# Batch 0's mixing beside the position tables, key terms on four column groups, first stacks and tables in turn

## The chip, the cores and the metric

The kernel runs on one core of a Trainium2 chip, as one launch. The metric is the device time of the launch in microseconds. Engines are named as the profile names them: PE is TensorE's matmuls, PEld its weight loads, DVE is VectorE, ACT is ScalarE, POOL is GpSimd, SP is SyncE, which only issues DMAs.

## What is computed

One block of a vision tower on x of shape (32, 512, 256, 4): a mixing over the last two axes, attention with relative position terms in two directions (32 batches, 512 positions, 16 heads of 16), and a layer of eight experts. What the change touches:

```python
h = einsum('bhid,oi,od->bho', x, weighted_sum, weight)
n = layernorm(h)
q, k, v = n @ Wq + bq, n @ Wk + bk, n @ Wv + bv      # 16 heads of 16
re = layernorm(rel_emb) * ln_g + ln_b                # 128 positions
pos_k, pos_q = re @ Wpk + bpk, re @ Wpq + bpq
scores = (q k^T + take(q pos_k^T, rel) + take(k pos_q^T, -rel)^T) / sqrt(48)
ctx = softmax(scores) @ v
h = h + ctx @ Wo + bo
```

## The kernel before

The program is a row of stages, each one or more blocks; a block ends when all its engines have ended and its last transfers have landed. B is 32 batches, P is 128, QT = 4 tiles of 128 positions make a batch's S = 512, HC = 2 chunks of 128 make the H = 256 channels, NH is 16 heads.

**Tables** (first block of `project`, L222 to L328). SP issues 19 loads (L226) and then the inputs of batches 0 and 1 (L229), 2 MB each. DVE waits for all 19 loads, takes the statistics of the embedding (L257), makes the mixing weights (eight products of 128x256, L262, into `mix`), normalizes, and goes on in turns with PE: transposes (L307), projections (L312), end and table matmuls (L319, L320), then DVE splits the tables into three bf16 parts (L276 to L292), PE makes the low rows (L324) and the bias of the key terms (L326), DVE splits the low rows, SP stores (L233, L235). PE has nothing else to do in this block.

**Projection loop** (second block of `project`, from L363). For each batch n PE does, in this order: `turn` (transposes of the normalized rows, L415), then for each of four tiles the mixing of batch n + 1 (L404: eight matmuls of 128x128 weights and 256 columns into `m_h[:, t]`) with a quarter of the q and k projections (L425) between the tiles, then `key_terms` (L433) and `project_v` (L442, two halves that share `m_v`). Ahead of the loop PE mixes batch 0, in four tiles on its own. A matmul in the program on fp32 data is two MATMULs in the profile. Key terms are 32 rows (two sides of 16 heads) by 512 positions: a projection of `full_k` with `kterm_w`, written to 32 partitions. ACT evicts them twice (L507, L508), POOL subtracts (L555), DVE splits (L610, L612). ACT also evicts h (L477) and q and k; DVE takes statistics and normalizes the next batch (L583), for which POOL takes a power (L537). SP's order within a batch is fixed: input of batch n + 2 (L371), h (L374), v (L376), then, when the last part is split, 12 DMAs of the parts (L383, L384) and 2 of the key terms (L386, L387).

**Attention** (`attend`, from L706). For each of 512 heads: `tables` (PE multiplies the head's rows in `stack` with `tabs`, L859), ACT evicts them to `skew_in` (L941, two buffers), SP writes them to a ring in HBM (L738) and reads them back skewed (L750) into `bias`, POOL (L809, L818, L827) and DVE (L995) fill and mask, PE adds up the scores (L871, L873, L878), DVE adds the rest of the bias and takes the maximum (L1010, L1017), PE turns them (L887), ACT takes the exponential (L947), PE multiplies with the values (L900, four heads into four groups of 32 output partitions). Tables are made LEAD = 5 heads ahead, read back NEXT = 3 heads ahead; `stack` has SR = 8 slots of SH = 2 heads. `load_stack` and the other issues of SP stand in one order written out by hand. Before the loop SP loads the constants (L709 to L717), waits until DVE has set the ones rows of all eight slots (L982, L983), loads seven slots and the values, and then writes tables 0 to 4, with reads 0 to 2 after writes 2 to 4. PE waits for all constants and all ones.

**Output and experts** follow; the change does not touch them.

Of the kernel before, what the change touches and what calls it, by code (L numbers as in the profile page):

```python
# [17 lines left out]
BF16 = mybir.dt.bfloat16  # L18
I32 = mybir.dt.int32
U32 = mybir.dt.uint32  # L20
ALU = mybir.AluOpType
# [3 lines left out]
P = 128  # L25
# [128 lines left out]
def project(nc, io, B, ctx, sem, passed, d_tab, d_plain, d_stack, d_kterm, d_v, d_h):  # L154
# [12 lines left out]
    kterm_bias = sb("kterm_bias", [2 * NH, 1])  # L167
# [3 lines left out]
    x_in = [sem(f"p_x_in{u}") for u in range(2)]  # L171


    with ExitStack() as tctx:
# [3 lines left out]
        def tps(name, shape):  # L178
# [22 lines left out]
        t_tab = tps("tab", [P, 2 * HC, S])  # L201
        t_end = tps("end", [P, 2, HC, 2])
        t_low = tps("low", [2 * NH, 2 * TW])
        t_in, t_const, t_dve, t_pe, t_pool, t_out = (
            sem("t_" + n) for n in ("in", "const", "dve", "pe", "pool", "out"))
        loads = [
            (ws, io["wsT"].rearrange("(c p) o -> p c o", p=P)),
            (wd, io["tok_weight"].partition_broadcast(P)),
# [13 lines left out]
        with nc.Block() as block:  # L222
            @block.sync
            def _(sp):
                for dst, src in loads:
                    sp.dma_start(dst[:], src).then_inc(t_in, 16)  # L226
                for u in range(2):

                    sp.dma_start(xt[:, u], xT[u].rearrange("d (c p) s -> p (d c) s", p=P)).then_inc(x_in[u], 16)  # L229
# [15 lines left out]

            @block.vector
            def _(dve):
# [7 lines left out]

                dve.wait_ge(t_in, 16 * len(loads))
# [3 lines left out]
                for d in range(ND):  # L260
                    for c in range(HC):
                        nc.vector.tensor_tensor(mix[:, d * HC + c], ws[:, c], wd[:, d], ALU.mult)  # L262
# [41 lines left out]
            def _(pe):  # L304
                pe.wait_ge(t_dve, 6)
                for c in range(HC):
                    mm = pe.transpose(t_turn[:, c * P:(c + 1) * P], rel[:, c * P:(c + 1) * P], ident[:])  # L307
                mm.then_inc(t_pe, 1)
                pe.wait_ge(t_dve, 7)
# [4 lines left out]
                mm.then_inc(t_pe, 1)  # L314
                pe.wait_ge(t_dve, 8)
# [5 lines left out]
                mm.then_inc(t_pe, 1)  # L321
                pe.wait_ge(t_dve, 19)
                for c in range(HC):
                    pe.matmul(t_low[0:NH, 0:TW], own_low[:, c], tab_q[:, c], start=(c == 0), stop=(c == HC - 1))  # L324
                for c in range(HC):
                    mm = pe.matmul(t_low[:, TW:TW + 1], kterm_w[:, c], consts[:, 0, c, 0:1], start=(c == 0),  # L326
                                   stop=(c == HC - 1))
# [14 lines left out]
    full_t = sb("full_t", [2 * NH, S])  # L342
    part_t = sb("part_t", [2 * NH, 3, S], BF16)
    v_sb = sb("v_sb", [P, QT, NH, VROW])
    m_h = ps("m_h", [P, QT, H])
# [3 lines left out]
    m_t = ps("m_t", [2 * NH, S])  # L349
# [13 lines left out]
    with nc.Block() as block:  # L363
# [33 lines left out]
        def _(pe):  # L397
            def mixing(n, i, u, t):
# [7 lines left out]
                if t % 2:  # L406
                    mm.then_inc(h_done, 1)
# [52 lines left out]
            for t in range(QT):  # L460
                mixing(0, 0, 0, t)
# [1255 lines left out]
```

## Time and profile before

| | us |
|---|---|
| median of 3 runs (lowest, highest) | 5222.62 (5219.48, 5224.54) |
| profiled execution, its own time | 5222.77 |
| its span, first to last instruction | 5220.9 |
| tables and stores, to the next block | 0 to 48.1 |
| projection block | 48.1 to 977.1 |
| one batch in it (transposes begin at 887.52 and 915.71) | 28.2 |
| attention block | 977.1 to about 4350 |
| output, choice of rows and experts | to 5220.9 |

The launch adds 1.9 us to the span. The granted clock of TensorE is 0.945 of full on the mean, 0.50 in the stretches in which it had been idle. In the views below, times are from the span's start; "idle before" is the time the engine stood still ahead of a group, and the name behind the arrow is what ended it.

### The profile page before, as it was taken

The numbers are of one execution on the slowest core, as the hardware profiler recorded it, in microseconds if no ns is written. First come the engines' busy times: TensorE is split into PE (matmuls) and PEld (weight loads), VectorE is DVE, ScalarE is ACT, GpSimd is POOL, SyncE is SP. The second block draws the span as 40 slices with busy tenths as digits, with TensorE's granted clock in tenths as the row PEclk, the third lists the DMA queues.
The fourth block names the chain that finished last, engine by engine and source line by source line (L and its number), as shares of the span: only waits on it lengthen the run. The fifth ranks groups of instructions, "written<-read, shape, count | busy, mean of one in ns | idle before, by whom it ended". The sixth has DMA issues, their size and how long they took to land. (4 is left out here: it accounts for less than half of the span.)

```text
span 5220.9 us, 110891 instructions
## 1 busy us (share of the span) xinstructions
PE 4618.7 (88%) x31272; PEld 3293.2 (63%) x31272; DVE 3524.1 (67%) x9058; ACT 2584.8 (50%) x4809; POOL 1925.2 (37%) x4461
## 2 busy tenths in 40 slices
PE   6999999499999999999999999999999996771698
PEld 4666666276666666666666666666666664661565
DVE  3333333388888878888878878888888885775511
ACT  1222222266666666666666666666666661110011
POOL 1222222144444444444444444444444443550022
PEclk9999999799999999999999999999999997885599
DMA  4766767699999999999999999999999995771033
GB/s 137 237 225 223 235 223 231 212 349 353 351 340 348 343 331 351 346 336 347 343 328 344 353 332 342 345 337 346 339 342 344 350 340 168 250 241 61 9 90 73
DMA packets 672172, 1461.31 MB, mean 280 GB/s; under 512 B 48195, under 2 KB 290291, under 8 KB 671603
## 3 DMA queue, kind: packets, MB, share of 16 engines
q1 hardware_dynamic: 665462, 1446.22, 81.7%
q0 software_dynamic: 6144, 8.52, 1.0%
q8 instruction: 236, 3.87, 0.3%
q14 instruction: 330, 2.70, 0.2%
HBM read 738.61 MB, written 715.94 MB: 279 GB/s over the span
## 5 line engine op out<-in xcount | busy, mean ns | idle before, releaser
L1010 DVE CUSTOM_DVE_ANT_1 a_scored<-a_ps_m_s,a_bias 128x512 f32<-128x512 f32 x2048 | 1397.5, 682 | 575.2 <-PE a_ps_m_s L878 543.5
L947 ACT ACTIVATE a_probsT<-a_ps_m_t 128x512 f32<-128x512 f32 x2048 | 1227.1, 605 | 938.3 <-PE a_ps_m_t L887 936.3
L887 PE MATMUL a_ps_m_t<-a_ident,a_scored 128*128 128x128 f32 x8192 | 1264.5, 277 | 0.5 <-ACT a_probsT L947 0.5
L941 ACT ACTIVATE a_skew_in<-a_ps_m_tab 128x512 f32<-128x512 f32 x2048 | 1125.7, 614 | 199.7 <-DMA d_skew<-a_skew_in 140.5
L887 PEld LDWEIGHTS a_ps_m_t<-a_ident,a_scored 128*128 128x128 f32 x8192 | 938.9, 141 | 437.3 <-DVE a_scored L1017 352.1
L1017 DVE TENSOR_SCALAR a_scored<-a_scored,a_top_of 128x512 f32<-128x512 f32 x2048 | 1045.2, 530 | 0.0
L827 POOL TENSOR_SCALAR_AFFINE_SELECT a_bias<-a_bias 128x128 f32<-128x128 f32 (+2 forms) x2560 | 980.5, 410 | 71.9 <-POOL a_bias L827 63.1
L818 POOL COPY a_bias<-a_high 128x128 f32<-128x128 f32 (+1 forms) x1024 | 355.9, 376 | 1764.9 <-DMA a_bias<-d_skew 1763.6
L878 PE MATMUL a_ps_m_s<-a_ident,a_bias 128*128 128x128 f32 x5120 | 902.6, 273 | 0.0
L859 PE MATMUL a_ps_m_tab<-a_tabs,a_stack 96*128 96x256 bf16 (+1 forms) x4096 | 714.2, 276 | 192.5 <-ACT a_skew_in L941 122.2
L878 PEld LDWEIGHTS a_ps_m_s<-a_ident,a_bias 128*128 128x128 f32 x5120 | 683.4, 142 | 109.0 <-issue 3.1
L873 PE MATMUL a_ps_m_s<-a_stack 99*128 99x512 bf16 (+2 forms) x2048 | 701.5, 343 | 45.5 <-issue 25.4
L859 PEld LDWEIGHTS a_ps_m_tab<-a_tabs,a_stack 96*128 96x128 bf16 (+1 forms) x4096 | 336.6, 98 | 411.0 <-ACT a_skew_in L941 344.7
L995 DVE COPY_PREDICATED a_bias<-a_ps_m_past,a_high 128x384 f32<-128x384 int32 x1024 | 544.1, 586 | 37.5 <-POOL a_high L809 34.0
L900 PE MATMUL a_ps_m_ctx<-a_probsT,a_values 128*17 128x512 f32 x4096 | 542.7, 602 | 1.2 <-ACT a_ctx_sb L953 1.2
L404 PE MATMUL p_ps_m_h<-p_mix,p_xt 128*128 128x256 f32 x2048 | 465.3, 381 | 7.3 <-PEq L222 7.3
L404 PEld LDWEIGHTS p_ps_m_h<-p_mix,p_xt 128*128 128x128 f32 x2048 | 388.7, 191 | 99.0 <-issue 51.9
L873 PEld LDWEIGHTS a_ps_m_s<-a_stack 99*128 99x128 bf16 x2048 | 200.6, 98 | 120.4 <-issue 64.5
L871 PE MATMUL a_ps_m_s<-a_stack 102*128 102x128 bf16 (+1 forms) x1024 | 254.7, 249 | 0.0
L1190 PE MATMUL o_ps_m_o<-o_wo,o_ctxn 128*128 128x256 f32 x512 | 166.8, 498 | 68.1 <-POOL o_ctxn L1156 68.0
L547 POOL TENSOR_TENSOR p_rest_q<-p_full_q,p_part_q 128x512 f32<-128x512 f32 x64 | 90.4, 1412 | 329.2 <-ACT p_part_q L496 329.2
L1190 PEld LDWEIGHTS o_ps_m_o<-o_wo,o_ctxn 128*128 128x128 f32 x512 | 128.6, 257 | 97.2 <-POOL o_ctxn L1156 40.4
(182 smaller groups left out, 3641.8 us busy)
## 6 DMA issues: line engine op xcount, KB each, us to landing
d_skew<-a_skew_in SPq DMA_DIRECT2D x1024, 480.0 KB, 7.7
a_bias<-d_skew SPq DMA_DIRECT2D x512, 896.0 KB, 8.9
a_stack<-d_stack SPq DMA_DIRECT2D x256, 384.0 KB
p_xt<-in_xT SPq DMA_DIRECT2D x32, 2048.0 KB, 9.2
d_ctx<-a_ctx_sb SPq DMA_DIRECT2D x128, 256.0 KB, 7.7
d_stack<-p_part_q SPq DMA_DIRECT2D x64, 384.0 KB, 2.8
d_stack<-p_part_k SPq DMA_DIRECT2D x64, 384.0 KB, 3.4
d_v<-p_v_sb SPq DMA_DIRECT2D x32, 544.0 KB, 3.0
```

What stands on the lines that cost most here:

```text
L404: mm = pe.matmul(m_h[:, t], xt[:, u, k, t * P:(t + 1) * P], mix[:, k], start=(k == 0), stop=(k == ND * HC - 1))
L827: nc.gpsimd.affine_select(blocks(r + out[0], (out[1], count)), blocks(r + of, (2, count)), pattern=[[0, count], [-sign, P]], base=0, chann ...
L859: mm = pe.matmul(m_tab[:, w, k], stack[0:rows, g % SR, hh % SH, at:at + P], tabs[0:rows, w, hh], start=True, stop=True)
L873: pe.matmul(bank[:, far:], row[0:ST + 3, t * P:(t + 1) * P], row[0:ST + 3, S + far:], start=not far, stop=False, skip_group_check=True)
L878: mm = pe.matmul(bank[:, k * P:(k + 1) * P], bias[:, at], ident[:], start=False, stop=(k == near[-1]), is_transpose=True, skip_group_check ...
L887: mm = pe.transpose(m_t[:, k % 2, t * P:(t + 1) * P], scored[:, hh % SCORED, t, k * P:(k + 1) * P], ident[:])
L900: mm = pe.matmul(m_ctx[j * CROW:j * CROW + VROW], values[:, half, k, (g * GH + j) % (NH // 2)], turned_at(g, j, k), start=(k == 0), stop=( ...
L941: nc.scalar.activation(skew_in[:, u, w, 2 * half:2 * half + 2], m_tab[:, w], ACT.Identity).then_inc(tab_kept, 1)
L947: nc.scalar.activation(turned_at(hh // GH, hh % GH, k), m_t[:, k % 2], ACT.Exp, scale=SCALE).then_inc(turned, 1)
L995: nc.vector.copy_predicated(blocks(r + at, (step, QT - 1)), m_past[:, w].unsqueeze(1).to_broadcast([P, QT - 1, P]), high[:, v, w].unsqueez ...
L1010: nc.vector.tensor_tensor_reduce(split(scored[:, hh % SCORED, t]), split(m_s[:, t % 2]), extra, 1.0, -3.0e38, ALU.add, ALU.max, top_of[:, ...
L1017: nc.vector.tensor_scalar(at, at, top_of[:, hh % 2, t:t + 1], None, ALU.subtract).then_inc(lowered, 1)
```

## The change

**Tables.** The loads of the mixing's two factors come first, with a semaphore of their own; DVE makes `mix` when these two are there, ahead of its wait for the other loads. The input of batch 0 is issued from ACT's queue, that of batch 1 stays on SP behind the loads. PE mixes batch 0 in four tiles, one ahead of the transposes of L307, one ahead of L312, one ahead of L319 and one ahead of L324; the mixing ahead of the projection loop is gone. For this `m_h` is allocated before the tables, and `t_tab` has TW = 256 columns in place of 512.

**Key terms.** `m_t`, `full_t`, `part_t` are [128, 128]: positions 128j to 128j + 127 stand on partitions 32j to 32j + 31. The bias has 128 rows, made by four times as many one-column matmuls. The store takes eight DMAs in place of two.

**Attention.** The ones rows are set slot by slot, slots 0 to 3 by DVE (slot 0 first of all), 4 to 7 by POOL ahead of its other memsets. SP loads `past`, six of the twelve pieces of `tabs`, stack 0, the plain rows and the identity; the other six pieces are issued by ACT. Then stacks 1 and 2, writes 0 and 1, read 0, stack 3, write 2, read 1, stack 4, write 3, read 2, stack 5, write 4, stack 6, the values. POOL's parts of heads 0 to 2 come two tables earlier in its order.

```diff
-    kterm_bias = sb("kterm_bias", [2 * NH, 1])
+    kterm_bias = sb("kterm_bias", [P, 1])
+    def mix_tile(pe, u, t):
+        for k in range(ND * HC):
+            mm = pe.matmul(m_h[:, t], xt[:, u, k, t * P:(t + 1) * P], mix[:, k],
+                           start=(k == 0), stop=(k == ND * HC - 1))
+        if t % 2:
+            mm.then_inc(h_done, 1)
...
-        t_tab = tps("tab", [P, 2 * HC, S])
+        t_tab = tps("tab", [P, 2 * HC, TW])
...
+                sp.dma_start(ws[:], io["wsT"].rearrange("(c p) o -> p c o", p=P)).then_inc(t_mix, 16)
+                sp.dma_start(wd[:], io["tok_weight"].partition_broadcast(P)).then_inc(t_mix, 16)
                 for dst, src in loads:
                     sp.dma_start(dst[:], src).then_inc(t_in, 16)
-                for u in range(2):
-                    sp.dma_start(xt[:, u], xT[u].rearrange("d (c p) s -> p (d c) s", p=P)).then_inc(x_in[u], 16)
+                sp.dma_start(xt[:, 1], xT[1].rearrange("d (c p) s -> p (d c) s", p=P)).then_inc(x_in[1], 16)
...
+            @block.scalar
+            def _(act):
+                act.dma_start(xt[:, 0], xT[0].rearrange("d (c p) s -> p (d c) s", p=P)).then_inc(x_in[0], 16)
...
+                dve.wait_ge(t_mix, 32)
+                for d in range(ND):
+                    for c in range(HC):
+                        nc.vector.tensor_tensor(mix[:, d * HC + c], ws[:, c], wd[:, d], ALU.mult)
                 dve.wait_ge(t_in, 16 * len(loads))
...
+                pe.wait_ge(t_dve, 1)
+                pe.wait_ge(x_in[0], 16)
+                mix_tile(pe, 0, 0)
                 pe.wait_ge(t_dve, 6)
...
                 for c in range(HC):
-                    mm = pe.matmul(m_t[:], kterm_w[:, c], full_k[:, c], start=(c == 0), stop=(c == HC - 1))
+                    for j in range(QT):
+                        mm = pe.matmul(m_t[j * 2 * NH:(j + 1) * 2 * NH], kterm_w[:, c], full_k[:, c, j * P:(j + 1) * P],
+                                       start=(c == 0), stop=(c == HC - 1), skip_group_check=True)
                 mm.then_inc(t_done, 1)
...
-                    sp.dma_start(to[:, 0:3], part_t[0:NH]).then_inc(t_out, 16)
-                    sp.dma_start(to[:, 3:], part_t[NH:]).then_inc(t_out, 16)
+                    for j in range(QT):
+                        for side in range(2):
+                            at = (2 * j + side) * NH
+                            sp.dma_start(to[:, 3 * side:3 * side + 3, j * P:(j + 1) * P], part_t[at:at + NH]
+                                         ).then_inc(t_out, 16)
...
-            for t in range(QT):
-                mixing(0, 0, 0, t)
...
+            sp.dma_start(past[:], io["past"]).then_inc(past_in, 16)
+            load_tabs(sp, 0)
+            sp.wait_ge(ones_set, 1)
+            load_stack(0, 0)
+            sp.wait_ge(zeroed_p, 1)
+            sp.dma_start(tabs[ST + TERMS:, 1], d_plain).then_inc(const_in, 16)
+            sp.dma_start(ident[:], io["ident"]).then_inc(const_in, 16)
+            for g in range(1, SR - 1):
+                if g == 3:
+                    for m in range(2):
+                        write_tables(m, m, m)
+                    read_tables(0, 0, 0)
+                sp.wait_ge(ones_set if g < SR // 2 else ones_pool, g % (SR // 2) + 1)
                 load_stack(0, g)
+                if g >= 3 and g - 1 < LEAD:
+                    write_tables(g - 1, g - 1, g - 1)
+                    if g - 2 < NEXT:
+                        read_tables(g - 2, 0, g - 2)
+            sp.wait_ge(ones_pool, SR // 2)
             load_values(0, 0)
             load_values(0, 1)
-            for m in range(LEAD):
-                write_tables(m, m, m)
-                if m >= LEAD - NEXT:
-                    read_tables(m - LEAD + NEXT, 0, m - LEAD + NEXT)
...
+            for g in range(SR // 2, SR):
+                nc.gpsimd.memset(stack[ST:, g], 1.0).then_inc(ones_pool, 1)
+            pool.wait_ge(ones_pool, SR // 2)
...
+            nc.vector.memset(stack[ST:, 0], 1.0).then_inc(ones_set, 1)
             nc.vector.memset(tabs[ST:, 1], 0.0).then_inc(zeroed_p, 1)
             nc.vector.memset(m_ctx[:], 0.0).then_inc(zeroed_p, 1)
-            nc.vector.memset(stack[ST:, 0], 1.0).then_inc(zeroed_p, 1)
-            nc.vector.memset(stack[ST:, 1:], 1.0).then_inc(zeroed_p, 1)
+            for g in range(1, SR // 2):
+                nc.vector.memset(stack[ST:, g], 1.0).then_inc(ones_set, 1)
```

## Rows read from the trace of the kernel before

**Rows 1.** Busy us (x instructions) by engine, granted clock, DMA share, in four stretches.
```profile
100.00:940.00 840.00, 814.63 (x3218) 574.00 (x3217) 315.47 (x773) 241.71 (x389) 217.05 (x179) 1.00 0.70 227
977.00:1001.00 24.00, 0.00 (x0) 0.00 (x0) 16.34 (x5) 0.00 (x0) 0.89 (x5) 0.50 0.38 105
1001.00:1032.00 31.00, 10.73 (x40) 2.82 (x40) 0.61 (x2) 10.87 (x20) 3.00 (x11) 0.50 0.96 270
1100.00:4300.00 3200.00, 3028.87 (x23846) 2129.34 (x23844) 2634.21 (x6956) 2164.23 (x4096) 1384.42 (x3973) 0.99 1.00 343
```

**Rows 2.** Order of time, 0 to 70 us: start, length, what [idle before].
```profile
17.28 0.43 DVE L257 BATCH_NORM_STATS2 t_stats<-t_rel 128x6 f32<-128x256 f32 x1 [17.28 <-DMA p_qk_bias<-in_bk_col]
...
23.49 3.78 PE L312 MATMUL t_ps_pos<-t_wp,t_relT 128*128 128x256 f32 x8 [0.59 <-DVE t_relT L269]
...
28.13 0.38 PE L319 MATMUL t_ps_end<-t_ends,t_pos 128*128 128x2 f32 x2 [0.85 <-DVE t_pos L272]
...
38.03 0.69 DVE L292 COPY t_tab_q<-t_ps_tab 128x512 f32<-128x512 f32 x1
...
48.11 1.28 ACT L477 ACT_TABLE_LOAD   x1 [48.11 <-PEq L222]
...
48.15 15.81 PE L404 MATMUL p_ps_m_h<-p_mix,p_xt 128*128 128x256 f32 x64 [7.32 <-PEq L222]
...
57.09 0.60 ACT L477 ACTIVATE p_h_sb<-p_ps_m_h 128x512 f32<-128x512 f32 x1 [7.70 <-PE p_ps_m_h L404]
...
68.58 1.82 PE L415 MATMUL p_ps_m_turn<-p_ident,p_xn 128*128 128x128 f32 x8 [4.61 <-DVE p_xn L583]
```

**Rows 3.** Order of time, one batch of the projection loop, 880 to 917 us.
```profile
880.99 1.90 PE L433 MATMUL p_ps_m_t<-p_full_k,p_kterm_w 128*32 128x512 f32 x4
...
881.44 0.11 PEld L433 LDWEIGHTS p_ps_m_t<-p_full_k,p_kterm_w 128*32 128x32 f32 x1 [0.32 <-issue]
...
882.82 1.99 PE L442 MATMUL p_ps_m_v<-p_wv,p_xnT 128*128 128x256 f32 x8
...
883.29 1.01 POOL L537 TENSOR_TENSOR p_rstd<-p_var_eps,p_minus_half 128x4 f32<-128x4 f32 x1 [3.00 <-DVE p_var_eps L577]
...
885.55 1.38 DVE L583 TENSOR_SCALAR p_xn<-p_h_sb,p_moments,p_rstd 128x256 f32<-128x256 f32 x4
...
887.52 1.04 PE L415 MATMUL p_ps_m_turn<-p_ident,p_xn 128*128 128x128 f32 x8
...
900.92 0.42 SPq L371 DMA_DIRECT2D p_xt<-in_xT  x1
...
916.58 3.62 PE L404 MATMUL p_ps_m_h<-p_mix,p_xt 128*128 128x256 f32 x16
```

**Rows 4.** Costliest groups of the page: busy us, mean ns, then idle before.
```profile
L900 PE MATMUL a_ps_m_ctx<-a_probsT,a_values 128*17 128x512 f32 x4096 | 542.7, 602 | 1.2 <-ACT a_ctx_sb L953 1.2
```

**Rows 5.** DMA issues of the page: count, KB each, median us to landing.
```profile
p_xt<-in_xT SPq DMA_DIRECT2D x32, 2048.0 KB, 9.2
```

**Rows 6.** Order of time, end of the projection stage.
```profile
964.71 0.68 DVE L612 TENSOR_TENSOR p_part_t<-p_full_t,p_part_t 32x512 bf16<-32x512 f32 x1
...
974.77 0.43 SPq L387 DMA_DIRECT2D d_kterm<-p_part_t  x1
```

**Rows 7.** Order of time, start of the attention stage.
```profile
977.11 0.31 POOL L798 MEMSET a_bias<- 128x256 f32 x1 [16.48 <-POOLq L363]
...
978.00 7.85 SPq L714 DMA_DIRECT2D a_tabs<-d_tab  x12
...
985.08 12.01 DVE L983 MEMSET a_stack<- 9x14336 bf16 x1 [2.94 <-issue]
...
1004.08 15.17 SPq L738 DMA_DIRECT2D d_skew<-a_skew_in  x6
...
1019.29 1.72 SPq L750 DMA_DIRECT2D a_bias<-d_skew  x1
...
1032.49 0.61 PE L873 MATMUL a_ps_m_s<-a_stack 99*128 99x512 bf16 x1 [5.41 <-DVE a_bias L995]
```

**Rows 8.** Waits of 1100 to 4300 us: who for whom, us, times, longest.
```profile
ACT a_skew_in L941 <- DMA d_skew<-a_skew_in: 124.7, 164, 2.6
```

More of the change, by code:

```diff
@@ L324, in _ @@
                     pe.matmul(t_low[0:NH, 0:TW], own_low[:, c], tab_q[:, c], start=(c == 0), stop=(c == HC - 1))
-                for c in range(HC):
-                    mm = pe.matmul(t_low[:, TW:TW + 1], kterm_w[:, c], consts[:, 0, c, 0:1], start=(c == 0),
-                                   stop=(c == HC - 1))
+                for j in range(QT):
+                    for c in range(HC):
+                        mm = pe.matmul(t_low[j * 2 * NH:(j + 1) * 2 * NH, TW:TW + 1], kterm_w[:, c],
+                                       consts[:, 0, c, 0:1], start=(c == 0), stop=(c == HC - 1))
                 mm.then_inc(t_pe, 1)
@@ L359, in project @@
     DMAS = 2 * len(RUNS) * HC
+    TERM_DMAS = 16 * 2 * QT
     CH = 2 * HC
@@ L402, in mixing @@
                     after(pe, h_kept, 2 * (n - 1) + t // 2 + 1 if not isinstance(n, int) or n else 0)
-                for k in range(ND * HC):
-                    mm = pe.matmul(m_h[:, t], xt[:, u, k, t * P:(t + 1) * P], mix[:, k],
-                                   start=(k == 0), stop=(k == ND * HC - 1))
-                if t % 2:
-                    mm.then_inc(h_done, 1)
+                mix_tile(pe, u, t)
             def turn(n):
@@ L505, in keep_terms @@
                 after(act, parts_done, (CH + 1) * n)
-                after(act, t_out, 32 * n)
+                after(act, t_out, TERM_DMAS * n)
                 nc.scalar.activation(full_t[:], m_t[:], ACT.Identity, bias=kterm_bias[:])
@@ L700, in turned_at, with load_tabs @@
         return probsT[:, a, c]
+    def load_tabs(eng, w):
+        for j in range(SLOTS):
+            part = (SIDE_B if w == 0 else SIDE_A)[j]
+            eng.dma_start(tabs[j:ST:SLOTS, w], d_tab[w, part].rearrange("(h d) x -> d h x", d=HD)
+                          ).then_inc(const_in, 16)
     def early(b, hh, lag):
@@ L834, in _ @@
                 keep_high(m, m)
-                if m >= LEAD - NEXT:
-                    part(m - LEAD + NEXT, 0, m - LEAD + NEXT)
+                if 0 < m <= NEXT:
+                    part(m - 1, 0, m - 1)
             def body(b, last):
```

50 lines of the change are left out of this document (21 added, 29 removed).

## The prediction, made before the changed kernel was run

> **What bounds the kernel now.** I read the page first (engine shares, the 40 slices), then busy time by stage, then the order in time at the three places that the change edits, then the waits of the attention stage. [Rows 1] give the stages. In the projection loop (100 to 940 us) TensorE is busy 814.63 of 840 us at full clock while the DMA engines stand at 0.70: TensorE's own instruction stream is the bound, and what is cut from it per batch comes off 32 times. From 977 to 1001 TensorE does nothing and DMA stands at 0.38; from 1001 to 1032 TensorE is busy 10.73 of 31 us and DMA 0.96. In the attention loop both are full (TensorE 95%, DMA 1.00), so a start of attention that is earlier for TensorE alone may be partly handed back by the DMA engines. The start of the program is a serial chain too [rows 2]: tables end, then 64 mixing matmuls of batch 0 for 15.81 us, then 4.6 us of eviction and normalization, then the first transposes at 68.58.
>
> **Part 1, mixing of batch 0 beside the tables.** Removed after the tables: the 15.81 us of L404. What stays between the block's start and the transposes is a table load of 1.28, one more eviction of 0.6 (the first half's, hidden before) and the 4.6 us from last matmul to transposes: 6.5 us in place of 68.58 - 48.15 = 20.4, so -13.9.
> Added to the table chain: the four mixing tiles stand between its steps. In [rows 2] the eight L312 matmuls took 3.78 us, 0.47 each, on an engine that had been idle; a tile of 16 takes 3.62, 0.226 each, in the loop [rows 3]. Tile 0 then takes 8 x 0.47 + 8 x 0.226 = 5.6 us and starts after the statistics of L257 (0.45). The normalization of the embedding, formerly behind the products of L262 that now come earlier, is ready before the tile ends. Then the transposes (0.5), tile 1 (3.6), L312's eight at 0.226 (1.8), tile 2 (3.6): the table matmuls start 15.5 us after L257, where they were 28.13 - 17.28 = 10.9 after it: +4.7. Tile 3 (3.6) hides under the 7.7 us of VectorE work between the table matmuls and 38.72; of that cover half is enough. Twelve more one-column matmuls in the low step: +0.5, hidden by nothing. Bounds of this item: +2 (the clock is up early) to +8 (tile 0 wholly slow).
> The loads: the 2 MB of batch 0 now leave from ScalarE's queue at the start, and share the DMA engines with the 19 loads for which L257 waits. Below, 0 (they fit into gaps); above, 2 MB at the 343 GB/s of [rows 1], 6.1 us. I take 3.5, between the ends, since the loads had some slack and the transfers are served side by side. SP's own queue loses one issue and is not late; nothing is behind the ScalarE issue until the next block. The products of L262 now wait for two loads only and run before L257.
> Sum: -13.9 + 4.7 + 0.5 + 3.5 = -5.2, ends -11 and +1.
>
> **Part 2, key terms on four column groups.** [Rows 3]: the key-term matmuls start at 880.99 and project_v's at 882.82, 1.83 us per batch for four matmuls of 512 columns, 0.43 each. Now 16 matmuls of 128 columns, 0.107 each, in four groups of output partitions. Do such groups overlap? The context matmuls have the same form, 512 columns in four groups of output partitions: 4096 of them, 602 ns long each, keep TensorE busy 542.7 us [rows 4], 1.06 us for eight. Two in a row cost 0.86 by L433's pace and eight in a row 3.4, so four run at once, at 0.2 over. By that, four waves of 0.107 and 0.2 make 0.63. Saved: 1.2 us a batch, 38.4 over 32. Ends: 0.1 (no overlap, 16 x 0.107 = 1.71) and 1.3; a loss is a rival below.
> What is late next? The transposes of the next batch need the normalized rows, which need the power on GpSimd (883.29 + 1.01 = 884.30) and VectorE's L583 (885.55 to 886.93). TensorE reached the transposes (L415) at 887.52. L583 itself stands behind the eviction of project_v's first half, which moves with TensorE; it could begin at 884.35 at the earliest, so the transposes could come 1.7 us earlier before they wait. 1.2 passes.
> The stores: eight DMAs of 256 B runs in place of two of 1 KB runs, six more issues of 0.43 (0.5 with the gap) on SP, +3 us, less about 0.6 because the split before them (0.68 in [rows 6], and its cast) works on 128 columns in place of 512. Behind them on SP is the load of the batch after next, issued at 900.92, landing 9.2 us later [rows 5], at 910.1; its mixing starts at 916.58. Of 6.4 us of slack 2.4 and the 1.2 of the shorter batch go; 2.8 stay. Cost 0 in the loop.
> At the stage's end the cover is gone: the last parts were split at 965.39, the last issue came at 974.77 [rows 6], and attention began at 977.11. Six more issues +3.0, shorter split -0.6: +2.4. Ends +0.5 (the DMA engines were draining anyway) and +4.
> Runs of 256 B are what the Trainium skill warns of, in "DMA: Bandwidth & Descriptors", Specifications: below 512 B a transfer is read, changed and written back. No row here shows such a store; were each 48 KB then three times as dear, they would still be under a twentieth of a batch's bytes, and the sum would stand.
>
> **Part 3, start of attention.** Before [rows 7]: the block starts at 977.11, SP waits for VectorE's 12.01 us memset before its first stack load, the first table matmul starts at 1001 [rows 1], the first read of a table is issued at 1019.29, the first score matmul starts at 1032.49, that is 24, 42 and 55 us in.
> After: the memset is seven pieces of 12.01/7 = 1.7 us; VectorE does four, the tables' (1.8) and the PSUM one (0.5): 9.2 us. GpSimd does four; it has no such row, but its 128x256 memset took 0.31, so 2048 elements at that pace take 2.5, four 10. Below, VectorE's pace, 7; above, twice 2.5, if the two engines disturb each other, 20. Take 10: TensorE starts 10.3 in, 13.7 sooner. SP issues six table loads of 0.65 (7.85/12), the other six go out from ScalarE, whose evictions are not due before 11, then stack 0. The first written table leaves at 13, and no longer stands behind seven stack loads and the values in the DMA queues; it should land by 18 to 20 instead of waiting 15 us (1004.08 to 1019.29); read, mask, fill: first score about 31 to 33 in, 22 to 24 sooner. Behind SP's waits for written tables now stand the stacks 3 to 6 and the values; heads 6 on need those, and they come in time.
> But the DMA work up to steady state is the same, and DMA was 0.96 busy from 1001 on. It can be earlier only by its idle time in the first 31 us: 24 x 0.62 + 31 x 0.04 = 16, less what it idles now while the first tables are made, 2 to 5: 11 to 14. In the loop the DMA engines hold TensorE now and then: ScalarE waits 124.7 us for stored tables [rows 8]. So between 11 to 14 (DMA decides) and 22 to 24 (TensorE decides); nearer the first because the full DMA row says so: -15. Ends -5 and -24.
>
> **Sum.** -5.2 - 38.4 + 2.4 - 15 = -56.2 from the profiled execution's 5222.77, which is the median of the runs (5222.62) within 0.2: 5167.
>
> **Rivals.** (a) Attention gives nearly nothing back, because in a loop where DMA is at 1.00 the head start melts: -5.2 - 38.4 + 2.4 - 3 = -44.2, 5179. For it: [rows 1, 8]. Against: DMA idles 15 us now. (b) All of TensorE's head start stays, -24: 5158. (c) A floor per matmul: the groups are issued one after another at 0.107 us each, 1.7 in all, saving 0.1 a batch and 3 over the stage: 5202. Against: [rows 4], where eight would then have taken 3.4 us. The Trainium skill, "TensorEngine Tiling (Array Packing)", Instruction Overhead, speaks for a mild form of it: some 60 cycles for each matmul, so that a factor should not be taken from a dimension that is small; an estimate by that page is 12 x 60 cycles at 2.4 GHz, 0.3 us a batch, and 5176. (d) Slower: in TensorE's stream at the key terms each 128-column matmul also waits for its own weights, which L433 shows at 0.11 each. 16 x (0.107 + 0.11) = 3.5 us in place of 1.83, +1.64 a batch, +52.5: 5222.8 + 52.5 - 17.8 = 5257. It decides from 2.7 us per batch on ((17.8 + 10.4)/32 is 0.9 more than now). Against: [rows 4] again. (e) The first part does not do what it says: load contention and tiles eat the gain, +1 instead of -5.2: 5173.
>
> **Numbers.** Forecast (5155 to 5173) 0.55; (a) 0.15, (b) 0.08, (c) 0.09, (d) 0.04, (e) 0.05, and 0.04 for waits that I do not see, half of them beyond the old time. A measurement of this kernel can tell 0.2%, 10.4 us, from no change. Range 5145 to 5198: it takes in (a), (b), (e), the skill's form of (c) and the bad ends of the terms one at a time; (c) in full, (d) and the unseen are left out. Faster 0.90 (all but (d) and the unseen, less a little for several terms at their bad ends), same 0.05, slower 0.05.
>
> **What would show it.** Table matmuls about 4 us later relative to L257, the first transposes at 62 to 64 us. Batch period 28.2 down to 27.0, 0.6 us from key terms to project_v; if it is 1.7, (c); over 2.7, (d). A wait of the mixing for its input would show the queue late. First table matmul 10 to 11 us after the block's start, first score 31 to 33; the attention loop's length, first score to last, grows by about 8 us if DMA decides and not at all under (b). I am wrong if the period stays at 28 or the transposes begin to wait for VectorE.

## The result, and the profile after it

The changed kernel took 5154.01 us (median of 4 runs, 5149.46 to 5173.15) beside 5221.05 us (4 runs) for the kernel before on the same chip: a ratio of 0.9883, 95% interval 0.9853 to 0.9913. That is 67 us less; 56 were forecast, and the two later comparisons of the same pair gave 0.9886 (0.9867 to 0.9905, 59 us) and 0.9892 (0.987 to 0.9914, 54 us). The profiled execution took 5149.46 us, its span is 5147.6 and the mean granted clock 0.947.

Busy time by stretch, the changed kernel; columns as in [rows 1]. The first line answers to the projection loop, the second to the attention loop, the other three to the start of attention, whose block begins at 934.85.

```profile
100.00:890.00 790.00, 764.68 (x3519) 566.88 (x3518) 301.07 (x762) 219.81 (x382) 193.34 (x177) 1.00 0.74 238
1040.00:4240.00 3200.00, 3037.04 (x23974) 2134.51 (x23973) 2650.80 (x6998) 2173.91 (x4114) 1398.88 (x3998) 1.00 1.00 345
934.00:946.00 12.00, 0.00 (x0) 0.00 (x0) 9.01 (x6) 0.00 (x0) 7.92 (x9) 0.50 0.95 189
946.00:960.00 14.00, 7.53 (x28) 2.03 (x28) 0.63 (x2) 6.51 (x12) 0.38 (x2) 0.50 0.79 199
960.00:971.00 11.00, 3.25 (x13) 1.18 (x14) 1.05 (x2) 3.75 (x8) 2.44 (x8) 0.50 0.99 316
```

Both loops look as before: TensorE is busy 97% of the projection loop and 95% of the attention loop, and DMA is full in the second. The stages became shorter or began earlier; none got another bound. The new thing is the third line: DMA engines 95% busy in the first 12 us of attention, where they had stood at 0.38 for 24 us, yet moving only 189 GB/s.

The start of the program, order of time, the changed kernel [rows 2]. L273 is the old L257, L178 the mixing.

```profile
0.81 0.52 ACTq L256 DMA_DIRECT2D p_xt<-in_xT  x1
...
9.53 2.77 DVE L271 TENSOR_TENSOR p_mix<-t_ws,t_wd 128x256 f32<-128x256 f32 x8 [9.53 <-DMA t_wd<-in_tok_weight]
...
22.14 0.43 DVE L273 BATCH_NORM_STATS2 t_stats<-t_rel 128x6 f32<-128x256 f32 x1 [9.83 <-DMA p_qk_bias<-in_bk_col]
...
22.62 5.51 PE L178 MATMUL p_ps_m_h<-p_mix,p_xt 128*128 128x256 f32 x16 [22.62 <-DVE t_stats L273]
...
28.18 3.62 PE L178 MATMUL p_ps_m_h<-p_mix,p_xt 128*128 128x256 f32 x16
...
31.64 1.89 PE L329 MATMUL t_ps_pos<-t_wp,t_relT 128*128 128x256 f32 x8
...
36.82 0.28 PE L337 MATMUL t_ps_end<-t_ends,t_pos 128*128 128x2 f32 x2
...
49.05 0.41 PE L346 MATMUL t_ps_low<-t_consts,p_kterm_w 128*32 128x1 f32 x16
...
56.86 1.28 ACT L495 ACT_TABLE_LOAD   x1 [56.86 <-PEq L230]
...
63.45 1.97 PE L434 MATMUL p_ps_m_turn<-p_ident,p_xn 128*128 128x128 f32 x8 [14.00 <-DVE p_xn L601]
```

The statistics start 4.9 us later than before (22.14 for 17.28); the table matmuls 14.7 us after them (10.9 before, 15.5 forecast); the projection block at 56.86, and its transposes 6.6 us later (6.5 forecast) at 63.45 in place of 68.58.

One batch of the loop, order of time, the changed kernel [rows 3]; L453 is the old L433, L463 is `project_v`.

```profile
844.06 1.48 DVE L601 TENSOR_SCALAR p_xn<-p_h_sb,p_moments,p_rstd 128x256 f32<-128x256 f32 x4
...
845.99 1.04 PE L434 MATMUL p_ps_m_turn<-p_ident,p_xn 128*128 128x128 f32 x8
...
857.71 3.84 SPq L409 DMA_DIRECT2D d_kterm<-p_part_t  x8
...
861.89 0.42 SPq L391 DMA_DIRECT2D p_xt<-in_xT  x1
...
867.64 0.64 PE L453 MATMUL p_ps_m_t<-p_full_k,p_kterm_w 128*32 128x128 f32 x16
...
868.21 2.00 PE L463 MATMUL p_ps_m_v<-p_wv,p_xnT 128*128 128x256 f32 x8
```

`project_v` begins 0.57 us after the first key-term matmul, where it was 1.83. The single records start in fours, within 0.02 us of 867.65, 867.78, 867.89 and 868.00: four column groups run at once, a wave every 0.11 to 0.13 us. The transposes still follow `project_v` without a wait for the normalized rows: these end at 845.54, the transposes begin at 845.99.

The start of attention, order of time, the changed kernel [rows 7]. L826 and L1017 set the ones rows, L753 writes a table (old L738), L765 reads one (old L750), L736 loads a stack (old L721), L903 is a head's first score matmul (old L873).

```profile
929.59 3.72 SPq L409 DMA_DIRECT2D d_kterm<-p_part_t  x8
934.85 7.03 POOL L826 MEMSET a_stack<- 9x2048 bf16 x4 [16.57 <-POOLq L383]
...
934.85 4.03 ACTq L724 DMA_DIRECT2D a_tabs<-d_tab  x6
...
939.25 0.60 SPq L736 DMA_DIRECT2D a_stack<-d_stack  x1
...
944.54 1.76 DVE L1017 MEMSET a_stack<- 9x2048 bf16 x1 [0.38 <-issue]
...
947.61 1.03 PE L889 MATMUL a_ps_m_tab<-a_tabs,a_stack 96*128 96x256 bf16 x4 [29.24 <-DMA a_ident<-in_ident]
...
950.66 5.16 SPq L753 DMA_DIRECT2D d_skew<-a_skew_in  x4
...
956.86 0.86 SPq L765 DMA_DIRECT2D a_bias<-d_skew  x1
...
969.21 1.09 ACT L973 ACTIVATE a_skew_in<-a_ps_m_tab 128x512 f32<-128x512 f32 x2 [6.37 <-DMA d_skew<-a_skew_in]
...
970.75 0.63 PE L903 MATMUL a_ps_m_s<-a_stack 99*128 99x512 bf16 x1
```

First table matmul 12.8 us into the block (23.9 before), first write of a table 15.8 (27.0), first read 22.0 (42.2), first score 35.9 (55.4). Between the last two, ScalarE waits 6.4 us for stored tables.

**The trace as a ledger.** Each line: start of the embedding's statistics; first transposes; period of a batch; last transposes of the stage; attention block; first score after the block's start; first to last score; from there to the end.

| profiled execution | stat. | transp. | period | last tr. | block | score | loop | rest |
|---|---|---|---|---|---|---|---|---|
| before | 17.28 | 68.58 | 28.18 | 943.80 | 977.11 | +55.4 | 3289.6 | 898.8 |
| after | 22.14 | 63.45 | 26.92 | 899.75 | 934.85 | +35.9 | 3281.5 | 895.3 |

42.3 us are gained up to the attention block, 19.5 more by the first score. The rest, 11.5, comes from stretches in which the traces themselves scatter: over the 14 profiled executions of this study the attention loop took 3266 to 3296 us, whatever the kernel. So one pair of traces can't tell the attention part; the experiments have to. The first transposes scatter too: they come at 67.7 to 69.2 us in the three traces with the old start of the program, at 63.5 to 64.9 in the eight with the new one.

### The profile page after: what moved, and what is told of

It reads as the page before. It is cut to its first block and busy times, and to the rows that moved or that the text cites. A ratio compares the mean times of both kernels' runs of the same rounds, so it can differ in the third digit from the quotient of the medians.

```text
span 5147.6 us, 112220 instructions
## 1 busy us (share of the span) xinstructions
PE 4567.6 (89%) x31668; PEld 3287.6 (64%) x31668; DVE 3502.7 (68%) x9060; ACT 2564.7 (50%) x4809; POOL 1911.7 (37%) x4465
## 5 line engine op out<-in xcount | busy, mean ns | idle before, releaser
L903 PE MATMUL a_ps_m_s<-a_stack 99*128 99x512 bf16 (+2 forms) x2048 | 700.6, 342 | 30.1 <-issue 19.6
L178 PE MATMUL p_ps_m_h<-p_mix,p_xt 128*128 128x256 f32 x2048 | 466.0, 381 | 22.6 <-DVE t_stats L273 22.6
L178 PEld LDWEIGHTS p_ps_m_h<-p_mix,p_xt 128*128 128x128 f32 x2048 | 389.1, 191 | 113.8 <-issue 44.5
L903 PEld LDWEIGHTS a_ps_m_s<-a_stack 99*128 99x128 bf16 x2048 | 200.6, 98 | 103.4 <-issue 60.9
```

What stands on the lines that cost most here:

```text
L178: mm = pe.matmul(m_h[:, t], xt[:, u, k, t * P:(t + 1) * P], mix[:, k], start=(k == 0), stop=(k == ND * HC - 1))
L903: pe.matmul(bank[:, far:], row[0:ST + 3, t * P:(t + 1) * P], row[0:ST + 3, S + far:], start=not far, stop=False, skip_group_check=True)
```

## The experiments

All were timed beside the kernel before on the same chip: e1 to e4 on one chip (before: 5217.85 us, median of 23), e5 to e8 on a second (5211.57, of 11), e9 to e12 on a third (5212.7, of 11).

### The three parts, each alone, and all

**e1_terms**: the kernel before, with the key terms of the change only.

```diff
                 for c in range(HC):
-                    mm = pe.matmul(m_t[:], kterm_w[:, c], full_k[:, c], start=(c == 0), stop=(c == HC - 1))
+                    for j in range(QT):
+                        mm = pe.matmul(m_t[j * 2 * NH:(j + 1) * 2 * NH], kterm_w[:, c], full_k[:, c, j * P:(j + 1) * P],
+                                       start=(c == 0), stop=(c == HC - 1), skip_group_check=True)
```

> The kernel before with the key terms on four column groups (and their stores) alone. If groups overlap in waves: 0.6 us from the key terms to project_v in place of 1.83, batch period 26.9 to 27.0 us in place of 28.2, 32 x 1.25 less about 3 us of longer issue at the stage's end, so 36 to 39 us faster. If the gain of the whole change had come from elsewhere (an issue floor per matmul): under 10 us.

**e2_tables**: the kernel before, with the first stage of the change only.

```diff
+                mix_tile(pe, 0, 0)
                 pe.wait_ge(t_dve, 6)
...
-            for t in range(QT):
-                mixing(0, 0, 0, t)
```

> The kernel before with the mixing of batch 0 beside the tables alone. Theory: 4 to 6 us faster, the first transposes at about 63.4 us, L257's successor at about 22.1 us, of which 4.9 are load contention. Rival (the clock state that the tiles leave behind helps the next batches): over 8 us.

**e3_attention**: the kernel before, with the new start of attention only.

```diff
+            for g in range(1, SR - 1):
+                if g == 3:
+                    for m in range(2):
+                        write_tables(m, m, m)
+                    read_tables(0, 0, 0)
...
-            nc.vector.memset(stack[ST:, 1:], 1.0).then_inc(zeroed_p, 1)
+            for g in range(1, SR // 2):
+                nc.vector.memset(stack[ST:, g], 1.0).then_inc(ones_set, 1)
```

> The kernel before with the new start of attention alone. Theory A (TensorE's head start stays): first score 19 to 20 us sooner and the whole 18 to 24 us faster, the stretch from first to last score as long as before within 3 us. Theory B (the DMA engines decide): 11 to 15 us faster in all, and the stretch from first to last score 5 to 8 us longer than before.

**e4_after**: the whole change, no edit.

> The changed kernel once more beside the others. If the three parts add up, its gain is the sum of theirs within 5 us; with theory A for attention that is 62 to 69 us, with theory B 52 to 58 us.

| | median us | ratio (95%) | us less | transp. | period | block | score |
|---|---|---|---|---|---|---|---|
| e1_terms | 5172.42 | 0.9909 (0.989 to 0.9928) | 45.4 | 67.69 | 26.92 | 938.96 | +55.5 |
| e2_tables | 5211.49 | 0.9981 (0.9969 to 0.9993) | 6.4 | 63.64 | 28.18 | 972.43 | +55.2 |
| e3_attention | 5205.96 | 0.9978 (0.9967 to 0.9988) | 11.9 | 69.22 | 28.18 | 978.39 | +36.1 |
| e4_after | 5158.44 | 0.9886 (0.9867 to 0.9905) | 59.4 | 63.97 | 26.92 | 935.58 | +36.1 |

Each part gives its own columns of the trace and leaves the others alone, within the scatter of the first transposes, and the parts add up: 63.7 us by themselves, 59.4 together, no more apart than the intervals. The tables' part is as forecast. The key terms bring attention forward by 38.2 us in the trace, of which 0.9 is an earlier first transpose and not their doing: 39.1 us are gained between the first and the last transposes and 1.8 given back at the stage's end. The interval of the runs, 38 to 57 us, has that at its edge; their median lies above the 36 to 39 that were expected, and why it is 7 us more than the trace I can't say. The new attention start moves the first score by 19.3 us and the time by 12 (6 to 17). That is the 11 to 15 of theory B and under the 18 of theory A; but theory B's other sign, a loop 5 to 8 us longer, is not there: the loop of e3's trace is 10 us shorter than that of the kernel before. The 59.4 us of the whole lie between what the two theories had given it (52 to 58, 62 to 69).

### How the column groups run: e5_two_groups

The changed kernel with two groups of 256 positions in place of four of 128, and four stores.

```diff
-                    for j in range(QT):
-                        mm = pe.matmul(m_t[j * 2 * NH:(j + 1) * 2 * NH], kterm_w[:, c], full_k[:, c, j * P:(j + 1) * P],
+                    for j in range(2):
+                        mm = pe.matmul(m_t[j * 2 * NH:(j + 1) * 2 * NH], kterm_w[:, c], full_k[:, c, 2 * j * P:2 * (j + 1) * P],
```

> The changed kernel with the key terms on two column groups of 256 positions, stored by four DMAs. If groups run at once and members of a group in turn: 4 x 0.213 + 0.14 = 0.99 us from the key terms to project_v, batch period 27.34 us, about 0.42 x 32 = 13 us slower than the changed kernel, less 2 us of issue at the stage's end. If the gain came from shorter evictions and splits behind the matmuls (they are half as short here) rather than from TensorE's stream, the period would lie between 26.92 and 27.1.

It took 5166.63 us (0.9902, 0.9874 to 0.9929), by the medians 11 to 14 us more than e6, e7 and e8, the changed kernel's other variants on the same chip. In its trace attention begins at 945.85, 10.3 us later than in e4's; 11 were expected. Order of time on TensorE, one batch of this kernel:

```profile
880.56 1.06 PE L453 MATMUL p_ps_m_t<-p_full_k,p_kterm_w 128*32 128x256 f32 x8
881.55 1.99 PE L463 MATMUL p_ps_m_v<-p_wv,p_xnT 128*128 128x256 f32 x8
```

`project_v` now comes 0.99 us after the key terms, and the period is 27.335 us. One group took 1.83 us (28.18), two 0.99 (27.34), four 0.57 (26.92): the cost is 0.15 us plus 1.68 divided by the number of groups, since both steps fit that line within 0.01 us. A cost per matmul that adds up over the groups would have shown as a smaller second step; four, eight and sixteen matmuls have the same 0.15. (All three come in four waves, so whether the 0.15 is paid once or by the wave stays open.) The evictions and splits behind the matmuls are shorter here too, but the period lies 0.42 us above the changed kernel's and so follows TensorE's step, not them.

The Trainium skill, "TensorEngine Tiling (Array Packing)", Instruction Overhead, has some 60 cycles of overhead on each matmul and advises against a factor from a small dimension. As a sum over matmuls of different column groups this does not hold here: by that estimate the twelve added matmuls would have cost 0.3 us more than the line gives. The page's own example, a matmul of one column that takes as long as one of 60, is a floor under each matmul, and pieces of 128 columns lie above it; the key-term runs don't test that. The Trainium skill, "DMA: Bandwidth & Descriptors", Specifications, says that below 512 B a transfer is read, changed and written back. The eight stores write 384 runs of 256 B a batch, 12,288 in all; the kernel before wrote 96 runs of 1 KB a batch. What the trace has of them are the key-term stores' own times from issue to landing, the changed kernel first, then the kernel before:

```profile
L409 SPq DMA_DIRECT2D d_kterm<-p_part_t x8: 315/316/332, 885.1 to 888.6; - x8
...
DMA to landing us min/median/max: 1.4/1.4/1.7
```

```profile
L386 SPq DMA_DIRECT2D d_kterm<-p_part_t x2: 332/332/332, 899.7 to 928.3; - x2
...
DMA to landing us min/median/max: 1.8/1.9/2.4
```

A store of a quarter of the bytes in 256 B runs lands in 1.4 us, one of 1 KB runs in 1.9. Per byte that is dearer, but nothing waits for it; a read and write-back can't be seen in these rows, nor excluded.

### The end of the stage: e6_tail

The changed kernel, with the last batch's eight stores of key terms issued by ScalarE, whose queue is empty by then.

```diff
-                            sp.dma_start(to[:, 3 * side:3 * side + 3, j * P:(j + 1) * P], part_t[at:at + NH]
-                                         ).then_inc(t_out, 16)
+                    if not (last and u):
+                        store_terms(sp, n)
...
             peeled(act, pairs, body)
+            act.wait_ge(parts_done, (2 * HC + 1) * B)
+            store_terms(act, B - 1)
```

> The changed kernel with the last batch's eight key-term stores issued from ScalarE's queue beside SP's stack stores. If the issues on SP set the end of the projection stage: attention begins 3 to 4 us sooner after the last transposes (35.1 us before it now, 31.5 then). If the DMA engines' drain sets it: 0 to 1 us.

5153.14 us, 0.9881 (0.9855 to 0.9907). Order of time, this kernel, end of the stage:

```profile
922.21 5.82 ACTq L386 DMA_DIRECT2D d_kterm<-p_part_t  x8
...
931.08 0.68 SPq L413 DMA_DIRECT2D d_stack<-p_part_k  x1
934.10 7.03 POOL L833 MEMSET a_stack<- 9x2048 bf16 x4 [14.27 <-POOLq L392]
```

The block starts 32.8 us after the last transposes, where it was 35.1: 2.3 us back, less than the 3 to 4 expected. Before the change it was 33.3 with key terms that were 1.26 us longer, so the change had cost 3.0. The issues are most of it: from the last split of the key terms to the block it is 11.7 us in the kernel before, 12.4 with two more issues (e5), 14.2 with six more, and 11.9 here. The run time, like those of e7 and e8, can't be told from the changed kernel's 0.9883 to 0.9892.

The rest is not in the issues. TensorE's busy time and clock in the last batch, and its eight q matmuls, in the kernel before and then in the changed one:

```profile
948.00:950.00 2.00, 2.00 (x6) 0.95 (x5) 0.00 (x0) 0.46 (x1) 0.00 (x0) 1.00 1.03 341
947.49 3.67 PE L425 MATMUL p_ps_m_qk<-p_xnT,p_wq 128*128 128x512 f32 x8 [2.65 <-issue]
```

```profile
904.00:906.00 2.00, 2.00 (x4) 0.89 (x3) 0.00 (x0) 0.00 (x0) 0.00 (x0) 0.50 1.03 345
902.86 5.37 PE L444 MATMUL p_ps_m_qk<-p_xnT,p_wq 128*128 128x512 f32 x8 [2.08 <-issue]
```

The granted clock is at its lower level (1.2 GHz, half of full) there, and the eight matmuls take 1.7 us longer. So it is in all ten traces with four column groups, e6's too, and in none of the four with one or two. TensorE had been idle for 2.1 us ahead of them, and for 2.65 us without a fall in the kernel before; why the clock falls there, no run here shows. The 3.0 us are then 2.5 for the issues and 1.7 for the clock, less 1.2, by difference, for shorter evictions and splits.

### The contention at the start: e7_order and e11_x_on_sync

**e7_order**: the changed kernel; the six loads that the tables don't need at once (wq, wk, wv and three biases) go behind the others and have a semaphore of their own, awaited where the bias is first used.

```diff
+                for dst, src in late:
+                    sp.dma_start(dst[:], src).then_inc(t_late, 16)
                 sp.dma_start(xt[:, 1], xT[1]
...
+                dve.wait_ge(t_late, 16 * len(late))
                 step(nc.vector.tensor_tensor(qk_bias[:, 2],
```

> The changed kernel with the six loads that only the projection needs (three weights, three biases) issued behind the others and waited for only before the first use of a bias. If load contention set the start of the tables: L257's successor at 15 to 17 us in place of 22.2 and the first transposes 5 to 7 us sooner, at 57 to 58.5. If mixing tiles or the input of batch 0 set it: under 2 us.

**e11_x_on_sync**: the changed kernel with batch 0's input on SP, behind the 19 loads, as in the kernel before.

```diff
-                act.dma_start(xt[:, 0], xT[0].rearrange("d (c p) s -> p (d c) s", p=P)).then_inc(x_in[0], 16)
+                act.wait_ge(t_mix, 32)
...
+                sp.dma_start(xt[:, 0], xT[0].rearrange("d (c p) s -> p (d c) s", p=P)).then_inc(x_in[0], 16)
                 sp.dma_start(xt[:, 1], xT[1]
```

> The changed kernel with batch 0's input issued on SP behind the 19 loads, as it was before. If contention on the DMA engines is what moved L257 from 17.3 to 22.2 us: its successor is back at 17.3, but tile 0 then waits for the input until 21 to 23 us, and the first transposes come within 1.5 us of the changed kernel's 64. If the queue itself mattered, the first transposes move by 3 us or more.

Order of time, start of e7_order, then of e11_x_on_sync:

```profile
19.39 0.43 DVE L278 BATCH_NORM_STATS2 t_stats<-t_rel 128x6 f32<-128x256 f32 x1 [7.47 <-DMA p_ident<-in_ident]
```

```profile
12.96 0.44 SPq L237 DMA_DIRECT2D p_xt<-in_xT  x1
...
17.79 0.43 DVE L274 BATCH_NORM_STATS2 t_stats<-t_rel 128x6 f32<-128x256 f32 x1 [9.01 <-DMA p_qk_bias<-in_bk_col]
...
23.30 6.39 PE L178 MATMUL p_ps_m_h<-p_mix,p_xt 128*128 128x256 f32 x16 [23.30 <-DMA p_xt<-in_xT]
```

e11 shows that the 4.9 us are the input's doing: taken off ScalarE's queue, the statistics start at 17.79 again, and even SP's issues are quicker (the 19 loads out by 12.9 us, by 17.0 in the changed kernel). But then mixing waits for its input until 23.30, and the transposes come at 64.73, as expected within 1.5 us of the changed kernel's: 0.8 later than the mean of the eight traces with the new start, and inside their range of 63.5 to 64.9. So the contention is the price of having the input early, and issuing it on ScalarE's queue bought about what it cost; 5157.78 us, 0.9898 (0.9878 to 0.9918), no difference to e12. e7 takes part of the contention back: the statistics at 19.39 and the transposes at 61.02, 2.9 us earlier than in e4's trace and outside the scatter, though 15 to 17 and 57 to 58.5 had been expected. The run time, 5155.31 us (0.988, 0.9853 to 0.9908), is too coarse for that.

### What decides the start of attention: e8_look and e10_loads_first

Two theories: TensorE's chain to the first score, or the DMA work that must be done before the loop runs at its pace.

**e8_look**: the changed kernel, four groups of stacks ahead in place of seven, so less DMA work before the first heads.

```diff
-            for g in range(1, SR - 1):
+            for g in range(1, LOOK):
...
-                        g = hh // SH + SR - 1
+                        g = hh // SH + LOOK
```

> The changed kernel with stacks loaded 4 groups ahead instead of 7, so that the start of attention moves 3 x 396 KB less before the third read. Theory B (the DMA work before steady state melts the head start): 1.2 MB at 235 to 345 GB/s is 3.5 to 5 us, so head 3 starts 3 to 5 us sooner and the whole is 3 to 5 us faster, first score unchanged. Theory A' (SP's order of waits for landed tables sets it): head 3 starts within 1 us of now and nothing is gained.

**e10_loads_first**: the changed kernel (its memsets and two queues kept) with SP's old order: seven stacks and the values first, then all writes and reads.

```diff
-                if g == 3:
-                    for m in range(2):
-                        write_tables(m, m, m)
-                    read_tables(0, 0, 0)
...
             load_values(0, 0)
             load_values(0, 1)
+            for m in range(LEAD):
+                write_tables(m, m, m)
+                if m >= LEAD - NEXT:
+                    read_tables(m - LEAD + NEXT, 0, m - LEAD + NEXT)
```

> The changed kernel with SP's old order at the start of attention (seven stacks and the values ahead of the first write of a table, reads 0 to 2 after writes 2 to 4), but with the new memsets by slot and the table loads on two queues. Theory B (the DMA work before steady state decides, not the order): first score 5 to 12 us later than in the changed kernel, but heads 10 to 64 within 3 us of it, and the whole within 4 us. Theory A (the interleaved order earns the gain): heads 10 to 64 stay as late as the first score, 5 to 12 us.

e8 took 5152.9 us (0.9877, 0.9851 to 0.9904), e10 5154.74 us (0.9888, 0.9866 to 0.991); neither time can be told from the changed kernel's. Mean start of the first VectorE addition to a head's scores, us after the block's start, over the traces that share a start:

| head | old start (3 traces) | new start (8) | e8, e9 (2) | e10 (1) |
|---|---|---|---|---|
| 0 | 56.5 | 37.2 | 37.2 | 45.0 |
| 1 | 62.7 | 46.9 | 44.6 | 51.2 |
| 3 | 74.7 | 64.9 | 60.5 | 61.8 |
| 5 | 86.8 | 75.8 | 71.7 | 75.3 |
| 12 | 130.6 | 119.7 | 115.2 | 118.3 |
| 64 | 459.0 (457.7 to 461.6) | 447.6 (442.9 to 454.1) | 442.1 | 448.5 |
| 256 | 1703.5 | 1689.0 (1678.0 to 1694.2) | 1685.7 | 1683.9 |
| 511, the last | 3337.6 (3333.4 to 3342.4) | 3319.7 (3310.3 to 3329.0) | 3309.9 | 3307.3 |

Of the head start of 19.3 us at head 0, 9.8 are left at head 3 and 11.4 at head 64. In e10 the first score comes 8 us later than in the changed kernel, and from head 3 on nothing is lost by it. Busy time by stretch says why; the kernel before, from its block's start at 977.11, then the changed kernel from 934.85, then e10 from 935.59, each for 24, 12 and 20 us:

```profile
977.11:1001.11 24.00, 0.06 (x1) 0.09 (x2) 16.34 (x5) 0.00 (x0) 0.89 (x5) 0.50 0.38 106
1001.11:1013.11 12.00, 5.27 (x20) 1.41 (x20) 0.00 (x0) 4.35 (x8) 0.38 (x2) 0.50 1.10 255
1013.11:1033.11 20.00, 6.02 (x23) 1.74 (x23) 1.05 (x2) 6.51 (x12) 2.63 (x9) 0.50 0.88 287
```

```profile
934.85:958.85 24.00, 6.44 (x24) 1.76 (x24) 9.63 (x7) 6.06 (x12) 8.30 (x11) 0.50 0.90 202
958.85:970.85 12.00, 4.20 (x17) 1.31 (x18) 1.05 (x2) 4.05 (x8) 2.44 (x8) 0.50 0.97 304
970.85:990.85 20.00, 12.75 (x68) 8.60 (x66) 12.24 (x33) 5.68 (x11) 6.66 (x22) 0.72 1.04 340
```

```profile
935.59:959.59 24.00, 5.34 (x20) 1.49 (x20) 9.63 (x7) 4.35 (x8) 8.30 (x11) 0.50 1.07 231
959.59:971.59 12.00, 4.30 (x16) 1.05 (x16) 0.00 (x0) 4.53 (x9) 0.19 (x1) 0.50 0.79 230
971.59:991.59 20.00, 10.68 (x64) 7.14 (x65) 10.94 (x30) 6.66 (x13) 10.34 (x32) 0.72 1.01 357
```

Length times the last column gives the bytes moved in 56 us: 2.5 + 3.1 + 5.7 = 11.3 MB before, 4.8 + 3.6 + 6.8 = 15.3 MB after, 5.5 + 2.8 + 7.1 = 15.4 MB in e10. The change is 4.0 MB ahead, 11.7 us at the 343 GB/s of the loop in [rows 1], and that is about the head start that is left from head 3 to head 64. e10 moves as many bytes and comes to the same place, however late its first score. So the gain comes from the loads that go out earlier, not from tables and stacks in turn, which move the first score and no more. In the kernel before, SP's first stack load stands behind the long memset, 20.0 us into the block:

```profile
997.11 0.35 SPq L721 DMA_DIRECT2D a_stack<-d_stack  x1
```

In the changed kernel it is issued 4.4 us in, and the table loads, on two queues, are out by then too (8.7 before). e10 keeps both, so no run here parts the memsets from the second queue. In e8 three stacks of 384 KB less stand ahead of the first heads, 1.2 MB or 3.4 us at that rate, and heads 3 to 64 come 4 to 5.5 us earlier, as theory B had it.

### The three together, and the change once more

**e9_all**: the edits of e6, e7 and e8 on the changed kernel. **e12_after_again**: the changed kernel, no edit.

```diff
+            store_terms(act, B - 1)
...
+                dve.wait_ge(t_late, 16 * len(late))
...
-            for g in range(1, SR - 1):
+            for g in range(1, LOOK):
```

> The changed kernel with the edits of e6, e7 and e8 together. If they add up: first transposes at about 61, projection's end 2.3 us sooner after the last transposes, heads from the third on 4 to 7 us sooner: 9 to 12 us faster than the changed kernel, and the fastest of all.

> The changed kernel once more, for comparison on the same chip: 0.988 to 0.989 of the kernel before.

e9 took 5149.86 us (5 runs, 5133.35 to 5156.13; 0.988, 0.9859 to 0.9901), e12 5158.54 us (5 runs, 5149.22 to 5164.82; 0.9892, 0.987 to 0.9914). In the trace each edit is in its place: transposes at 60.72 (63.59 in e12), the attention block at 929.86 (935.01), head 64 442.7 us after it (447.1), 9.6 us in sum, within the 9 to 12 expected. The medians are 8.7 us apart, but the intervals overlap: its median is the lowest one measured, its ratio is not (e8's is 0.9877), and its run times alone don't show that it beats the change. It beats the kernel before.

## Why the prediction came out

**Sum.** -56 was forecast; 67, 59 and 54 us were measured. The sum and its sign stand, and each part was found by itself, not only the total. Within the parts, terms that were off in opposite directions evened out, and that was luck.

**Part 1: -5.2; the trace pair shows -5.1 (63.45 for 68.58), the means of all traces -4.6, the runs of e2 -6.4.** The gain of 13.9 came as worked out. The terms added to the chain were off and evened out: contention 4.9 for 3.5, toward the upper bound of 6.1; the tiles 3.8 for 4.7; and the twelve more one-column matmuls under 0.1 for 0.5, since the block ends 8.75 us later in all. Tile 0 took 5.35 us to the next step where 5.6 was reckoned, its first eight matmuls at about 0.43 each and the others at 0.22; the transposes took 0.2 for 0.5, and each step behind them about 0.1 less. That the loads "had some slack" was the weak step: they are nineteen issues in a row, and beside e11's the changed kernel's end 4 us later. And the early input, which was the reason for the second queue, bought no clear time: by e11 the transposes come about 1 us later without it, within the scatter.

**Part 2: -38.4 and +2.4.** 1.26 us a batch for 1.2, by the pace read off the context matmuls in [rows 4]: the nearest row of the same form was the right one, though it stood in another stage. The transposes never waited for VectorE, as the slack of 1.7 had said. Behind SP's six more issues the load of `xt` still landed in time. At the stage's end, where that cover is gone, the cost was 3.0 for 2.4: the issues cost 2.5 in place of 3.0, the shorter splits and evictions gave back 1.2 in place of 0.6, and a term that the prediction doesn't have, the lower clock in the last batch, cost 1.7. That the sum came near is luck too.

**Part 3: -15; the runs of e3 show 12 (6 to 17).** The choice of DMA over TensorE was right: 19.3 us at the first score, 10 to 11 soon after. Two steps were off. The first table matmul was to come at 10.3 us and came at 12.8. GpSimd's memsets were quicker than thought (1.76 us for each, the price of VectorE's; 10 had been taken for four, 7.0 was measured). VectorE's were slower: its last one ended 11.5 us in, not 9.2, since it started 0.5 late and stood still for 0.4 ahead of four of them. And the constants came later still, the last of them landing just ahead of the matmul, in a stretch where DMA is 95% busy at 189 GB/s. I had priced the two engines' memsets and not the landing of the loads. The first score came at 35.9 in place of 31 to 33: 2.8 us of that were lost by the first write, which left at 15.8 in place of 13; it had landed 6.2 us later, as thought, and from the read to the score it was 13.9 us where 13 had been allowed. The sign that I had named, a loop longer by 8 us, was badly chosen: first to last score scatters over 30 us from trace to trace. Over the eight traces with the new start the gain stands at 11.4 us by head 64, 14.5 by head 256 and 17.9 by the last head, where the two groups of traces no longer overlap (3333 to 3342, 3310 to 3329). The bytes of the start explain the 11.4; what adds to it later in the loop, and why the runs of e3 show 12, stays open.

**The rivals.** (a), nothing but 3 us of attention: excluded by e3's interval. (b), all 24: excluded by it too, and by the heads. (c) and (d), groups one after another or behind their weights: 1.7 and over 2.7 us were to be seen, 0.57 was. The milder form of (c), 0.3 us a batch more, falls with the 0.57 and with e5. (e), the first part eaten up: e2 shows 6.4 us less (4 to 16 by the interval of its ratio).

## What to carry to other kernels

Where a matmul has few output columns in the array (32 of 128 here), splitting its free dimension over column groups cuts its time nearly by their number (1.83 us to 0.99 in two, 0.57 in four), even at 128 columns a piece; then look for what the added stores cost at the end of the stage, where nothing covers them, and at the granted clock there. At the start of a stage whose loop is bound by DMA, count bytes, not the first result: bytes moved by a given time, divided by the loop's rate, gave 12 us, which is what head 64 and the runs of e3 have, when the first score said 19. A load on a second queue slowed those of the first, and here the two evened out; what paid (3 us in e7's trace) was to put the loads that the chain doesn't need behind the others.

## What the runs showed of the hardware

- Sixteen 128-column fp32 matmuls in four column groups take 0.57 us to the next step, eight of 256 in two groups 0.99 (e5), four of 512 in one 1.83 (the kernel before).
- The 2 MB input issued at 0.81 us on ScalarE's queue landed after 14.3 us, and SP's 19 loads took until 17.0 us to issue in place of 12.9 (e11): here the issues themselves took longer while the DMA engines served another queue's transfer.
- A busy share of DMA is no rate: 0.95 with 189 GB/s in the first 12 us of attention, 0.97 with 304 and 1.00 with 345 later.
- In the last batch of the projection TensorE's clock is granted at half for 3.4 us in all ten traces with four column groups, and eight 512-column matmuls take 5.4 us in place of 3.7; the four traces with one or two groups don't have it.
- GpSimd sets nine rows of 2048 bf16 four times in 7.03 us, 1.76 each, and VectorE beside it takes the same 1.76.
